# LayerNorm statistics in the feed-forward of a two-layer transformer stage: plain fp32 product against two fp32r products of a split sum

## The chip, the core and the metric

The kernel runs on one NeuronCore of a Trainium2 chip. Five engines work side by side from their own instruction queues and meet at semaphores: TensorE (PE: matrix products and transposes, into PSUM), VectorE (DVE), ScalarE (ACT), GpSimd (POOL) and SyncE (SP, which starts DMAs). The metric is the device time of one execution in microseconds (us), from the first to the last instruction and a little around it.

## The reference

The input is (2, 1024, 256), 2048 tokens of 256 features. The program computes a softmax attention with a field term, a quaternion rotation, a mixture over 64 experts, and then two layers of window attention and feed-forward. The change lies in the feed-forward of these last two layers. There the reference computes, for each token:

```
h = shift_token(x)
mu = h.mean(-1, keepdims=True)
var = h.var(-1, keepdims=True)
h = (h - mu) / jnp.sqrt(var + 1e-05) * lg + lb
h = h @ w1 + b1
a, g = jnp.split(h, 2, axis=-1)
h = a * jax.nn.gelu(g, approximate=False)
x = x + h @ w2 + b2
```

x has 256 columns, w1 is 256 x 1364 and w2 is 682 x 256.

## The kernel before, in words

Activations are kept transposed: features on the 128 partitions (two blocks, KD = 2), tokens along the free dimension. The feed-forward works in units of 512 tokens, four in each layer (UNITS = 4), so u = 0 to 3 is layer 0 and u = 4 to 7 is layer 1. In the texts "unit n" is the n-th unit of its layer, and it normalises ahead for unit n + 1.

The statistics of a unit of tokens need a sum over 256 features. VectorE first adds the two blocks of 128 features (`tile_sums`, L2008, and for the squares `square_sums`, L2023). Then TensorE multiplies the 128 x 512 result with a 128 x 128 matrix that holds 1/256 everywhere (`means`, L1576, and `variances`, L1580), which leaves the mean, or the variance, in every partition. In between, VectorE subtracts the mean (`centred`, L2017) and ScalarE squares (L1837). After the variance ScalarE takes the root (`deviation`, L1842), VectorE the reciprocal in two halves (`inverse`, L2029), GpSimd multiplies (`normalise`, L1464), ScalarE scales and shifts (L1851), VectorE takes the high part (L2034) and GpSimd the low part (L1470).

All large products of the feed-forward are made of three products of fp32r parts (PRODUCTS: high by high, low by high, high by low). For each of six tiles f of the hidden layer TensorE makes the gate and value products (`hidden`, L1635, 12 matmuls for a tile, 6 for the last), ScalarE the gelu (L1923), and VectorE a chain of three: the product with the gate (L2111), a cast to fp32r for the high part (L2114) and a subtraction for the low part (L2116). Two PSUM banks take turns for the tiles, so tile f waits until the L2111 of tile f - 2 is over. Then L1747 makes the second product in two pieces, tiles 0 to 3 and tiles 4 and 5. The last piece waits for the low part of tile 5. VectorE adds the result to x (L2138).

The order on each engine is that of the code, written out by hand:

- VectorE, unit n: `tile_sums(u + 1)`; tile 0 of the hidden layer, `centred(u + 1)`; tile 1, `square_sums(u + 1)`; tile 2; tile 3, first half of `inverse`; tile 4, second half; tile 5; the high part of unit n + 1; the two additions of L2138.
- TensorE, unit n: tile 0 (for unit 0 already within the attention); `means(u + 1)` ahead of tile 1; tiles 1 to 3; `variances(u + 1)`; tiles 4 and 5; L1747.
- GpSimd, between two units: normalise and low part, and then in unit 0 of layer 0 two long subtractions for the next layer's weights (`low_qkv`, L1452), in unit 1 the scaling of the tables (L1242), and in layer 1 the addition of the layer's input (`with_input`, L1477).

In the attention of each layer the first unit (u = 0 and u = 4) is normalised in other buffers (names n_... instead of m_...), among the attention's own work.

Of the kernel before, what the change touches and what calls it, by code (L numbers as in the profile page):

```python
# [22 lines left out]
F32 = mybir.dt.float32  # L23
F32R = mybir.dt.float32r
BF16 = mybir.dt.bfloat16
ACT = mybir.ActivationFunctionType
ALU = mybir.AluOpType
# [3 lines left out]
P = 128  # L31
B, T, D = 2, 1024, 256
N = B * T
KD = D // P
TT = T // P
HALF = 512
# [1216 lines left out]
def stage_layers(nc, G, A, out):  # L1253


    with ExitStack() as ctx:
        sb = lambda n, s, dt=F32: ctx.enter_context(nc.sbuf_tensor(n, s, dt))
        sem = lambda n: ctx.enter_context(nc.semaphore(n))
# [9 lines left out]
        UNITS = NH * B  # L1268
# [6 lines left out]
        rn = sb("w_rn", [P, 2, 2, 2 * H1])  # L1275
        st = sb("w_st", [P, 2, 4, H1])
        rden = sb("r_rden", [P, TILES])
        mean = sb("m_mean", [P, P])
        eps = sb("m_eps", [P, 1])


        with ExitStack() as place:
            own = lambda n, s, dt=F32: place.enter_context(nc.sbuf_tensor(n, s, dt))
# [11 lines left out]
            oT = own("w_oT", [P, 2, HP, P])  # L1295
        with ExitStack() as place:
            own = lambda n, s, dt=F32: place.enter_context(nc.sbuf_tensor(n, s, dt))
            xc = own("m_xc", [P, KD, HALF])
            sqr = own("m_sq", [P, KD, HALF])
            xsum = own("m_xsum", [P, HALF])  # L1300
            sqsum = own("m_sqsum", [P, HALF])
            sd = own("m_sd", [P, HALF])
            rs = own("m_rs", [P, HALF])
            xn = own("m_xn", [P, KD, HALF])
            hn = own("m_hn", [P, KD, HALF])
            own("m_gap", [P, 2, KD, HALF])
            x1o = own("m_x1T", [P, NH, KD, HALF])
            own("m_gap0", [P, 2 * INNER])
            own("m_gap1", [P, VRING, INNER])
            with ExitStack() as inner:  # L1310
                on = inner.enter_context(nc.sbuf_tensor("r_on", [P, 2, D], F32))
            hids = [own(f"m_hid_{c}", [P, FT, HALF], F32R) for c in range(2)]
            gl = own("m_gl", [P, 2, HALF])
            hid = own("m_hid", [P, 2, HALF])
            hn_odd = own("m_hn_1", [P, 2, KD, HALF], F32R)
# [8 lines left out]
        def of_norm(u):  # L1324

            if u % UNITS == 0:
                return xc_first, sqr_first, xsum_first, sqsum_first, sqsum_first, xsum_first, xc_first, sqr_first
            return xc, sqr, xsum, sqsum, sd, rs, xn, hn
# [9 lines left out]
        consts, mu_ps, xc_done, xq_done, var_ps, sd_done, rs_done, xn_done, hn_done, hn_high, hn_low = (sem("m_" + n) for n in (  # L1338
            "consts", "mu_ps", "xc_done", "xq_done", "var_ps", "sd_done", "rs_done", "xn_done", "hn_done", "hn_high", "hn_low"))
        h_ps, gl_done, hid_done, hid_high, hid_low, y_ps, y_done = (sem("m_" + n) for n in (  # L1340
            "h_ps", "gl_done", "hid_done", "hid_high", "hid_low", "y_ps", "y_done"))
        w_copy, w_low, w_round, xsum_done, sqsum_done, stored = (sem("m_" + n) for n in (
            "w_copy", "w_low", "w_round", "xsum_done", "sqsum_done", "stored"))
        ld_half = [sem(f"m_ld_half{hf}") for hf in range(NH)]
# [6 lines left out]
        def mean_banks(u):  # L1351

            return (V_PS, V_PS) if u % UNITS == 0 else (PB[1][:, 0:HALF], PB[1][:, HALF:2 * HALF])
# [20 lines left out]
        def halves_swapped(rows):  # L1374

            (part, count), (one, _) = rows.ap
            return bass.AP(rows.tensor, rows.offset + C * one,
                           [(part, count), (INNER * one, 2), (HD1 * one, H1), (-C * one, 2), (one, C)])

        def tokens_shifted(q):  # L1380

            rows = xr[:, 0, q // (NW // 2), :]
            (part, count), (one, _) = rows.ap
            return bass.AP(rows.tensor, rows.offset + (1 + 2 * P * (q % (NW // 2))) * one,
                           [(part, count), ((B * (1 + T) - 1) * one, KD), (one, 2 * P)])

        def shifted(n, k):
            c0 = n % NH * HALF + (1 if k == 0 else 0)
            return xr[:, k, n // NH, c0:c0 + HALF]
# [23 lines left out]
        with nc.Block() as block:  # L1413
# [32 lines left out]
            def _(pool):  # L1446
                V = nc.gpsimd
# [11 lines left out]
                def normalise(u):  # L1459
                    xc, _, _, _, _, rs, xn, _ = of_norm(u)  # L1460
                    pool.wait_ge(rs_done, 2 * (u + 1))
                    pool.wait_ge(hn_done, KD * u)
                    for k in range(KD):
                        V.tensor_tensor(xn[:, k, :], xc[:, k, :], rs[:, :], ALU.mult).then_inc(xn_done, 1)  # L1464
# [64 lines left out]
                            low_piece(l, t - 6)  # L1529

                V.memset(xr[:, :, :, 0:1], 0.0).then_inc(zeroed, 1)
                V.memset(mean[:, :], 1.0 / D).then_inc(consts, 1)
                V.memset(eps[:, :], LN_EPS).then_inc(consts, 1)
                pool.wait_ge(consts, 2)
                attention(0)
                normalise(1)
                norm_low(1)
# [15 lines left out]
            def _(pe):  # L1553
                mm, tr = nc.tensor.matmul, nc.tensor.transpose
# [9 lines left out]
                def rotate(n):  # L1564
                    pe.wait_ge(x1_done, 4 * n + 4)
                    for m in range(KD):
# [4 lines left out]
                                      start=(k == 0), stop=(k == KD - 1))  # L1571
                        last.then_inc(rot_ps, 1)

                def means(u):
                    pe.wait_ge(xsum_done, u + 1)
                    mm(mean_banks(u)[0], mean[:, :], of_norm(u)[2][:, :], start=True, stop=True).then_inc(mu_ps, 1)  # L1576

                def variances(u):
                    pe.wait_ge(sqsum_done, u + 1)
                    mm(mean_banks(u)[1], mean[:, :], of_norm(u)[3][:, :], start=True, stop=True).then_inc(var_ps, 1)  # L1580

                def project(l, out_ps, i, j):
                    for n, (ch, cw) in enumerate(PRODUCTS):
# [187 lines left out]
                pe.wait_ge(x1_done, TILES)  # L1771
                pe.wait_ge(rot_out, KD * (N // HALF))
                attention(0, EARLY_SLOTS)
                pe.wait_ge(consts, 2)
                feed_forward(0)
                attention(1, EARLY_SLOTS)
                feed_forward(1)
# [181 lines left out]
            def _(dve):  # L1959
                V = nc.vector  # L1960
# [34 lines left out]
                def inverse_norms(l, q):  # L1995
                    dve.wait_ge(n_sqrt, NG // 2 * l + q + 1)
                    dve.wait_ge(turn_done, NG * l + max(2 * q - 2, 0))
                    V.reciprocal(rn[:, q % 2, :, :], nrm[:, :, :]).then_inc(rn_done, 1)

                def tile_sums(u):  # L2000
                    l, n = u // UNITS, u % UNITS
                    dve.wait_ge(wo_done, NG * l + 4 * (n + 1))
                    dve.wait_ge(mu_ps, u)
                    if n == 0:
                        dve.wait_ge(xn_done, KD * u)
                    if n == 1:
                        dve.wait_ge(add_done, NG * (l + 1))
                    V.tensor_tensor(of_norm(u)[2][:, :], shifted(n, 0), shifted(n, 1), ALU.add).then_inc(xsum_done, 1)  # L2008

                def centred(u):  # L2010
                    dve.wait_ge(mu_ps, u + 1)
# [7 lines left out]
                def square_sums(u):  # L2019
                    dve.wait_ge(xq_done, KD * (u + 1))  # L2020
                    dve.wait_ge(var_ps, u)
                    _, sqr, _, sqsum, *_ = of_norm(u)
                    V.tensor_tensor(sqsum[:, :], sqr[:, 0, :], sqr[:, 1, :], ALU.add).then_inc(sqsum_done, 1)  # L2023

                def inverse(u, q):
                    dve.wait_ge(sd_done, u + 1)
# [146 lines left out]
def program(nc, A, out):  # L2173


    with ExitStack() as top:
# [76 lines left out]
        sb("weights_kept", [P, WEIGHTS])  # L2253
        moe.close()
        stage_layers(nc, G, A, out)


# [76 lines left out]
```

## Time and profile before

| | |
|---|---|
| three runs | 1533.12, 1534.72, 1535.19 us; median 1534.72 us |
| profiled execution, own time | 1532.85 us |
| its span | 1531.1 us, 24499 instructions |
| TensorE | busy 1465.6 us (96%), mean granted clock 0.992 |
| VectorE | busy 1033.9 us (68%) |
| ScalarE | busy 902.2 us (59%) |
| GpSimd | busy 495.1 us (32%) |

Busy time of TensorE is modelled up to the end of each matmul, which the next one overlaps: how fast the matmuls really follow each other is seen in the distance between the starts. The two feed-forward stages are at about 1100 to 1220 us and 1424 to 1531 us. A plain fp32 product of 128 x 128 by 128 x 512 stands in the trace as two matmul instructions with two weight loads, an fp32r product as one.

### The profile page before, as it was taken

How to read it: one execution, taken by the hardware profiler on the slowest of the kernel's cores; microseconds unless marked ns; L12 is line 12 of the kernel's file. 1: busy time of each engine (PE TensorE's matmuls, PEld its weight loads, DVE VectorE, ACT ScalarE, POOL GpSimd, SP SyncE). 2: the span in 40 equal slices, each digit the busy share in tenths (PEclk: the TensorE clock that was granted, in tenths of full speed). 3: DMA queues.
4: the chain of work that ended last, by engine and by line, in shares of the span. 5: the costliest groups of instructions: out<-in, count | busy, mean ns of one | idle time of the engine just before them, and what ended most of it. 6: DMA issues, size and time to landing. Idle time of an engine off the chain costs nothing. (4 is left out here: it accounts for less than half of the span.)

```text
span 1531.1 us, 24499 instructions
## 1 busy us (share of the span) xinstructions
PE 1465.6 (96%) x9004; PEld 960.0 (63%) x9004; DVE 1033.9 (68%) x1855; ACT 902.2 (59%) x1888; POOL 495.1 (32%) x323
## 2 busy tenths in 40 slices
PE   8889999999998899999999999999999899998998
PEld 3432222222224679888887668877777678887776
DVE  3768888888844455656565567776597577676685
ACT  5137777777775442534343278988543388987341
POOL 7200000000003410000004177887343378886222
PEclk9999999999999999999999999999999999999999
DMA  8930232110000313030305120000200100000010
GB/s 246 170 41 2 43 42 41 24 22 2 1 12 15 104 38 111 14 110 0 124 0 149 42 73 2 2 1 1 77 7 0 59 2 1 2 1 29 14 42 28
DMA packets 59477, 64.85 MB, mean 42 GB/s; under 512 B 15154, under 2 KB 48706, under 8 KB 59380
## 3 DMA queue, kind: packets, MB, share of 16 engines
q1 hardware_dynamic: 58020, 60.17, 15.7%
q10 hardware_dynamic: 1360, 3.41, 0.6%
q8 instruction: 58, 0.95, 0.3%
q14 instruction: 39, 0.32, 0.1%
HBM read 52.88 MB, written 10.49 MB: 41 GB/s over the span
## 5 line engine op out<-in xcount | busy, mean ns | idle before, releaser
L581 DVE TENSOR_REDUCE mcol<-bank 128x1 f32<-128x1024 f32 x256 | 302.1, 1217 | 56.5 <-PE bank L572 56.5
L669 ACT ACTIVATE a_pt<-bank 128x512 f32<-128x512 f32 x512 | 266.5, 602 | 89.1 <-PE bank L701 89.1
L701 PE MATMUL bank<-qa,ka 99*128 99x512 bf16 x512 | 193.7, 386 | 7.6 <-ACT a_pt L669 3.8
L572 PE MATMUL bank<-ka,qa 96*128 96x512 bf16 x512 | 192.7, 384 | 4.4 <-DVE mcol L581 1.4
L2045 DVE CUSTOM_DVE_ANT_0 w_sm<-bank,mask,w_rn 128x256 f32<-128x256 f32 (+1 forms) x256 | 104.1, 463 | 80.2 <-PE bank L1627 79.5
L701 PEld LDWEIGHTS bank<-qa,ka 99*128 99x128 bf16 x512 | 49.2, 98 | 165.7 <-ACT a_pt L669 121.3
L1585 PE MATMUL bank<-wqkv,w_hst 128*128 128x512 f32 x576 | 150.3, 405 | 2.7 <-DVE w_sinp L1984 2.3
L1878 ACT ACTIVATE w_sm<-w_sm,w_st 128x256 f32<-128x256 f32 (+1 forms) x256 | 124.2, 490 | 22.3 <-DVE w_st L2045 22.0
L712 PE MATMUL bank<-a_pt,vst 128*32 128x512 f32 x1024 | 136.4, 605 | 0.1
L1485 POOL TENSOR_TENSOR w_sm<-w_sm,w_st 128x1024 f32<-128x1024 f32 (+1 forms) x64 | 115.4, 1803 | 20.2 <-DVE w_st L2052 20.0
L1585 PEld LDWEIGHTS bank<-wqkv,w_hst 128*128 128x128 f32 x576 | 104.2, 189 | 25.8 <-issue 5.1
L618 POOL COPY vst<-v 128x512 f32<-128x512 f32 x8 | 4.9, 615 | 334.0 <-PE bank L712 279.5
L1076 PE MATMUL bank<-f_y,f_ET 128*128 128x256 f32 x768 | 108.7, 290 | 0.7 <-DVE f_y L1175 0.7
L1076 PEld LDWEIGHTS bank<-f_y,f_ET 128*128 128x128 f32 x768 | 96.1, 191 | 3.9 <-issue 1.6
L1033 PE MATMUL bank<-phi,X0T 128*128 128x512 f32 x384 | 92.1, 394 | 4.6 <-PEq L768 4.6
L1494 POOL TENSOR_TENSOR w_cosp<-w_qkr,cosT 128x1024 f32<-128x1024 f32 x32 | 76.5, 2392 | 54.2 <-ACT w_qkr L1815 27.2
L1007 PE MATMUL bank<-f_th,X 128*128 128x512 f32 x384 | 90.3, 389 | 0.0
L572 PEld LDWEIGHTS bank<-ka,qa 96*128 96x128 bf16 x512 | 49.7, 99 | 60.5 <-DVE mcol L581 11.3
L1033 PEld LDWEIGHTS bank<-phi,X0T 128*128 128x128 f32 x384 | 73.0, 191 | 20.6 <-issue 5.4
L1923 ACT ACTIVATE m_gl<-bank,b 128x512 f32<-128x512 f32 (+1 forms) x48 | 33.1, 689 | 85.8 <-PE bank L1635 85.7
L742 POOL CAST phi<-phi 128x1024 fp32r<-128x1024 f32 x5 | 5.2, 1042 | 240.3 <-PE bank L1033 150.5
L1007 PEld LDWEIGHTS bank<-f_th,X 128*128 128x128 f32 x384 | 72.1, 188 | 14.9
(254 smaller groups left out, 2846.4 us busy)
## 6 DMA issues: line engine op xcount, KB each, us to landing
f_wex<-in_W SPq DMA_DIRECT2D x8, 2048.0 KB, 12.1
qa<-q_parts SPq DMA_DIRECT2D x48, 128.0 KB, 4.7
ka<-k_parts SPq DMA_DIRECT2D x48, 128.0 KB, 5.0
q_parts<-p_parts SPq DMA_DIRECT2D x16, 192.0 KB, 3.2
k_parts<-p_parts SPq DMA_DIRECT2D x8, 384.0 KB, 3.4
wqkv_raw<-in_wqkv SPq DMA_DIRECT2D x2, 1536.0 KB, 6.9
w_raw<-in_w SPq DMA_DIRECT2D x2, 1408.0 KB, 5.9
phi<-in_phi SPq DMA_DIRECT2D x5, 512.0 KB, 3.8
```

Of the source, the lines that this page charges most:

```text
L572: last = nc.tensor.matmul(max_bank(G, r)[:, jh * HALF:(jh + 1) * HALF], G["qa"][k][0:KS, hg % 2, h, it * P:(it + 1) * P], G["ka"][k][0:KS, ...
L581: nc.vector.reduce_max(G["mcol"][hg % 2][:, p:p + 1], max_bank(G, r)[:, :], X).then_inc(G["max_free"], 1)
L669: nc.scalar.activation(pt[n % 2][:, q, :], sbank(HG * step + q), ACT.Exp, scale=HD0 ** -0.5).then_inc(p_ready, 1)
L701: mm(sbank(i), ka[k][:, q, n * P:(n + 1) * P], qa[k][:, ih, q, :], start=True, stop=True).then_inc(st_ps, 1)
L712: last = mm(obank[32 * q:32 * q + 32, :], vst[hg // 2 % 2][:, jt, q, :], pt[jt % 2][:, q, :], start=(jt == 0), stop=(jt == TT - 1))
L1007: last = mm(PB[2 + b][:, k * HALF:(k + 1) * HALF], X0[cx][:, b * TT + mt, k * P:(k + 1) * P], ths[ct][:, mt % 2, :], start=(mt == n == 0), ...
L1033: last = mm(logit_bank(mt)[:, b * HALF:(b + 1) * HALF], X0T[cx][:, k, b * T + mt * P:b * T + (mt + 1) * P], phis[cp][:, k, :], start=(n == ...
L1076: last = mm(PB[1][:, HALF * (t % 2):HALF * (t % 2) + D], ETs[ce][:, t % 2, n, :], ys[cy][:, n, t // TT, :], start=(n == i == 0), stop=(n = ...
L1485: V.tensor_tensor(sm[:, i % 2, hs, keys(i)], sm[:, i % 2, hs, keys(i)], st[:, i % 2, 3, hs].unsqueeze(2).to_broadcast([P, 4, 2 * WIN if i ...
L1585: last = mm(out_ps, hst[:, i // 2 % 2, ch, k, (i % 2) * P:(i % 2 + 1) * P], wqkv[cw][:, k, j * INNER:(j + 1) * INNER], start=(n == k == 0) ...
L1878: last = S(sm[:, i % 2, h, keys(i)], sm[:, i % 2, h, keys(i)], ACT.Exp, bias=st[:, i % 2, 1, h:h + 1], scale=-1.0, accum_out=st[:, i % 2, ...
L2045: V.tensor_tensor_reduce(sm[:, s, h, keys(i)], S_PS[h % 2][:, c0:c0 + 2 * WIN][:, keys(i)], mask_of(i), rn[:, i // 2 % 2, s, h:h + 1], HIG ...
```

## The change

For three units in each layer (all but the first, u % 4 > 0) the sum and the sum of squares are split on VectorE into a high part (cast to fp32r) and a low part (the sum minus the high part), and TensorE makes two fp32r matmuls that add up in PSUM instead of one fp32 matmul. Each of the new VectorE instructions waits by semaphore for the one ahead of it. The matrix of 1/256 becomes fp32r: GpSimd fills a scratch tile and copies it over, once. The first unit of each layer stays as it was. The parts lie in a buffer that was a gap.

```diff
@@ stage_layers
-        mean = sb("m_mean", [P, P])
+        mean = sb("m_mean", [P, P], F32R)
...
-            own("m_gap", [P, 2, KD, HALF])
+            sum_parts, square_parts = (own(f"m_{n}_parts", [P, 2, HALF], F32R) for n in ("sum", "square"))
@@ GpSimd
-                V.memset(mean[:, :], 1.0 / D).then_inc(consts, 1)
+                V.memset(oT[:, 0, 0, :], 1.0 / D).then_inc(consts, 1)
                 V.memset(eps[:, :], LN_EPS).then_inc(consts, 1)
                 pool.wait_ge(consts, 2)
+                V.tensor_copy(mean[:, :], oT[:, 0, 0, :]).then_inc(consts, 1)
@@ TensorE
+                def of_tokens(bank, u, whole, parts):
+                    if u % UNITS == 0:
+                        return mm(bank, mean[:, :].bitcast(F32), whole[:, :], start=True, stop=True)
+                    mm(bank, mean[:, :], parts[:, 0, :], start=True, stop=False)
+                    return mm(bank, mean[:, :], parts[:, 1, :], start=False, stop=True)
+
                 def means(u):
                     pe.wait_ge(xsum_done, u + 1)
-                    mm(mean_banks(u)[0], mean[:, :], of_norm(u)[2][:, :], start=True, stop=True).then_inc(mu_ps, 1)
+                    of_tokens(mean_banks(u)[0], u, of_norm(u)[2], sum_parts).then_inc(mu_ps, 1)
...
-                    mm(mean_banks(u)[1], mean[:, :], of_norm(u)[3][:, :], start=True, stop=True).then_inc(var_ps, 1)
+                    of_tokens(mean_banks(u)[1], u, of_norm(u)[3], square_parts).then_inc(var_ps, 1)
@@ VectorE
+                def in_parts(u, whole, parts, whole_done, high_done):
+                    v = u - u // UNITS
+                    dve.wait_ge(whole_done, v)
+                    V.tensor_copy(parts[:, 0, :], whole[:, :]).then_inc(high_done, 1)
+                    dve.wait_ge(high_done, v)
+                    return V.tensor_tensor(parts[:, 1, :], whole[:, :], parts[:, 0, :].bitcast(F32), ALU.subtract)
...
-                    V.tensor_tensor(of_norm(u)[2][:, :], shifted(n, 0), shifted(n, 1), ALU.add).then_inc(xsum_done, 1)
+                    whole = V.tensor_tensor(of_norm(u)[2][:, :], shifted(n, 0), shifted(n, 1), ALU.add)
+                    if n:
+                        whole.then_inc(sums_whole, 1)
+                        in_parts(u, of_norm(u)[2], sum_parts, sums_whole, sums_high).then_inc(xsum_done, 1)
+                    else:
+                        whole.then_inc(xsum_done, 1)
```

`square_sums` is changed in the same way.

VectorE, start of unit 1 of layer 0, up to the subtraction of the mean (m_xsum: sum over the two blocks; m_xc: after the mean is subtracted). Before:

```order
L2138 SCALAR_TENSOR_TENSOR xr<-bank,b,xr 128x512 x2
L2008 TENSOR_TENSOR m_xsum<-xr 128x512
L2111 SCALAR_TENSOR_TENSOR m_hid<-bank,b,m_gl 128x512
L2114 CAST m_hid<-m_hid 128x512
L2116 TENSOR_TENSOR m_hid<-m_hid 128x512
L2017 TENSOR_TENSOR m_xc<-xr,bank 128x512 x2
```

Now:

```order
L2166 SCALAR_TENSOR_TENSOR xr<-bank,b,xr 128x512 x2
L2026 TENSOR_TENSOR m_xsum<-xr 128x512
L2013 CAST m_sum_parts<-m_xsum 128x512
L2015 TENSOR_TENSOR m_sum_parts<-m_xsum,m_sum_parts 128x512
L2139 SCALAR_TENSOR_TENSOR m_hid<-bank,b,m_gl 128x512
L2142 CAST m_hid<-m_hid 128x512
L2144 TENSOR_TENSOR m_hid<-m_hid 128x512
L2040 TENSOR_TENSOR m_xc<-xr,bank 128x512 x2
```

The cast and the subtraction stand between the sum and tile 0's chain, and the mean's matmul is released by the subtraction, no longer by the sum.

TensorE, the same unit, between the end of tile 0 and the first products of tile 1 (w_0 and w_1: high and low part of w1). Before:

```order
L1635 MATMUL bank<-m_hn,w_0 128x512 x4
L1635 MATMUL bank<-m_hn,w_1 128x512 x2
L1576 MATMUL bank<-m_xsum,m_mean 128x512
L1635 MATMUL bank<-m_hn,w_0 128x512 x4
L1635 MATMUL bank<-m_hn,w_1 128x512 x2
```

Now:

```order
L1644 MATMUL bank<-m_hn,w_0 128x512 x4
L1644 MATMUL bank<-m_hn,w_1 128x512 x2
L1580 MATMUL bank<-m_sum_parts,m_mean 128x512
L1581 MATMUL bank<-m_sum_parts,m_mean 128x512
L1644 MATMUL bank<-m_hn,w_0 128x512 x4
L1644 MATMUL bank<-m_hn,w_1 128x512 x2
```

The place of the mean's product is the same; all products of tile 1 and after stand behind it in TensorE's queue, and so behind its wait.

## Rows read from the trace of the kernel before

**Rows 1.** Busy time: window, length, PE, PEld, DVE, ACT, POOL (counts), clock, DMA, GB/s

```profile
1127.42:1154.11 26.69, 26.54 (x106) 19.63 (x107) 23.77 (x28) 12.90 (x15) 12.02 (x8) 1.00 0.00 1
```

**Rows 2.** Chain that ended last, unit 0 of layer 0: start, us, what

```profile
1099.07 0.69 DVE m_xsum L2008
1099.77 0.14 issue
...
1109.49 0.76 DVE m_hid L2111
...
1118.42 1.68 DVE m_hid L2116
...
1120.14 3.63 PE bank L1747 x12
```

**Rows 3.** Timeline of TensorE's weight loads around L1580: start, us, operation, idle before

```profile
1108.99 0.42 PEld L1580 LDWEIGHTS bank<-m_sqsum,m_mean 128*128 128x128 f32 x2
1109.65 0.19 PEld L1635 LDWEIGHTS bank<-n_hn,w 128*128 128x128 f32 x1 [0.24 <-issue]
1110.08 3.90 PEld L1635 LDWEIGHTS bank<-n_hn,w 128*128 128x128 f32 x17 [0.24 <-issue]
```

**Rows 4.** Timeline of VectorE, layer 0

```profile
1100.45 0.43 DVE L2114 CAST m_hid<-m_hid 128x512 fp32r<-128x512 f32 x1
1100.91 0.69 DVE L2116 TENSOR_TENSOR m_hid<-m_hid 128x512 fp32r<-128x512 f32 x1
...
1124.47 2.80 DVE L2008 TENSOR_TENSOR m_xsum<-xr 128x512 f32<-128x512 f32 x1
...
1127.97 2.92 DVE L2114 CAST m_hid<-m_hid 128x512 fp32r<-128x512 f32 x1
...
1137.03 0.75 DVE L2111 SCALAR_TENSOR_TENSOR m_hid<-bank,b,m_gl 128x512 f32<-128x512 f32 x1
...
1152.00 1.82 DVE L2008 TENSOR_TENSOR m_xsum<-xr 128x512 f32<-128x512 f32 x1
```

**Rows 5.** Timeline of VectorE, layer 1

```profile
1448.76 0.68 DVE L2008 TENSOR_TENSOR m_xsum<-xr 128x512 f32<-128x512 f32 x1
1451.14 0.75 DVE L2111 SCALAR_TENSOR_TENSOR m_hid<-bank,b,m_gl 128x512 f32<-128x512 f32 x1 [1.69 <-PE bank L1635]
```

**Rows 6.** Timeline of GpSimd, layer 0

```profile
1123.22 7.39 POOL L1452 TENSOR_TENSOR wqkv<-wqkv_raw,wqkv 128x1536 fp32r<-128x1536 f32 x2
...
1153.23 1.72 POOL L1242 TENSOR_TENSOR cosT<-cosT,qks 128x512 f32<-128x512 f32 x1
1154.92 1.29 POOL L1242 TENSOR_TENSOR sinT<-sinT,qks 128x512 f32<-128x512 f32 x1
```

**Rows 7.** Timeline of GpSimd, layer 1

```profile
1448.92 1.68 POOL L1477 TENSOR_TENSOR m_x1T<-m_x1T,xr 128x512 f32<-128x512 f32 x1 [0.35 <-DVE xr L2138]
```

**Rows 8.** Timeline of TensorE, layer 0's feed-forward

```profile
1099.90 1.10 PE L1576 MATMUL bank<-m_xsum,m_mean 128*128 128x512 f32 x2 [1.21 <-DVE m_xsum L2008]
...
1123.69 3.05 PE L1635 MATMUL bank<-m_hn,w 128*128 128x512 f32 x12
...
1141.76 5.75 PE L1747 MATMUL bank<-m_hid,w 128*128 128x512 f32 x24
...
1154.11 1.02 PE L1576 MATMUL bank<-m_xsum,m_mean 128*128 128x512 f32 x2
...
1204.33 7.37 PE L1747 MATMUL bank<-m_hid,w 128*128 128x512 f32 x24 [2.01 <-DVE w_sinp L1984]
```

**Rows 9.** Timeline of TensorE, layer 0's attention

```profile
1068.70 2.07 PE L1627 MATMUL bank<-w_kT,w_qT 64*128 64x256 f32 x8 [2.32 <-ACT w_qT L1859]
```

**Rows 10.** Timeline of TensorE, layer 1

```profile
1394.17 1.13 PE L1627 MATMUL bank<-w_kT,w_qT 64*128 64x256 f32 x8 [2.32 <-ACT w_qT L1859]
...
1450.87 1.02 PE L1576 MATMUL bank<-m_xsum,m_mean 128*128 128x512 f32 x2
```

**Rows 11.** Busy time after the idle gap of 2.01 us, columns as rows 1

```profile
1206.00:1208.00 2.00, 2.00 (x6) 1.51 (x6) 0.16 (x1) 0.00 (x0) 1.70 (x2) 0.50 0.00 0
```

More of the change, by code:

```diff
@@ L1341, in stage_layers @@
             "h_ps", "gl_done", "hid_done", "hid_high", "hid_low", "y_ps", "y_done"))
+        sums_whole, sums_high, squares_whole, squares_high = (sem("m_" + n) for n in (
+            "sums_whole", "sums_high", "squares_whole", "squares_high"))
         w_copy, w_low, w_round, xsum_done, sqsum_done, stored = (sem("m_" + n) for n in (
@@ L1773, in _ @@
                 attention(0, EARLY_SLOTS)
-                pe.wait_ge(consts, 2)
+                pe.wait_ge(consts, 3)
                 feed_forward(0)
@@ L2004, in tile_sums @@
                     if n == 0:
+                        dve.wait_ge(consts, 3)
                         dve.wait_ge(xn_done, KD * u)
@@ L2022, in square_sums @@
                     _, sqr, _, sqsum, *_ = of_norm(u)
-                    V.tensor_tensor(sqsum[:, :], sqr[:, 0, :], sqr[:, 1, :], ALU.add).then_inc(sqsum_done, 1)
+                    whole = V.tensor_tensor(sqsum[:, :], sqr[:, 0, :], sqr[:, 1, :], ALU.add)
+                    if u % UNITS:
+                        whole.then_inc(squares_whole, 1)
+                        in_parts(u, sqsum, square_parts, squares_whole, squares_high).then_inc(sqsum_done, 1)
+                    else:
+                        whole.then_inc(sqsum_done, 1)
                 def inverse(u, q):
```

## The prediction

> **What bounds the kernel now.** I read the chain of waits first, then the timelines of the three engines around the mean's product. TensorE is busy in 26.54 of the 26.69 us from one mean's product to the next, VectorE in 23.77 [rows 1], so the feed-forward looks like TensorE's. The chain says it is shared: sum on VectorE, mean and tiles 1 to 3 on TensorE, then from 1109.49 to 1120.1 VectorE alone (tiles 3, 4, 5 and two reciprocals), then the last piece of L1747 [rows 2]. So in every unit with a next one two things end last: how early tile 3's products are over, and what VectorE does from there to the low part of tile 5.
>
> **What TensorE saves.** In a steady run 17 weight loads of fp32r matmuls take 3.90 us from the first start to the last end; less the last one's 0.19, over 16 distances, that is 0.23 us each. The two loads of the fp32 variance begin at 1108.99 and end at 1109.41, so the second starts at about 1109.22; the next start at 1109.65 and 1110.08, so each of its two matmuls holds the engine for 0.43 us [rows 3]. Two fp32r matmuls take 0.47 us instead of 0.86, 0.39 us less. Twelve products: 4.7 us less work.
>
> The six variances save nothing of the end: they stand behind tile 3 of TensorE, and from tile 3 on the chain runs on VectorE, up to the point where L1747 waits for it [rows 2]. What TensorE wins there it waits for before the last piece. The six means stand ahead of tile 1 and count, if VectorE is in time.
>
> **What VectorE adds.** A cast of 128x512 takes 0.43 us and a subtraction 0.69 us in tile 0's chain; the second starts 0.03 us after the first's end [rows 4]. Behind a sum, with 0.04 us for the first wait: 1.19 us, twelve times, 14.3 us more on VectorE, and each mean's product is released that much later, at least. Queued behind the cast and the subtraction are tile 0's chain and the subtraction of the mean; queued behind TensorE's wait is tile 1 and all that follows.
>
> The six splits of the squares are hidden, as long as VectorE has idle time left (2.9 of 26.7 us in rows 1's window, the fullest): TensorE takes the variance only behind tile 3, and tile 3's chain starts when its products are over [rows 2], so what the split after tile 1 delays on VectorE has two tiles of TensorE to be caught up. I count nothing, with up to 0.3 us each as the other end, 1.8 us.
>
> **The sums, unit by unit.** Tile 3's chain starts 9.59 us after the mean's product (1099.90 [rows 8], 1109.49 [rows 2]); with fp32r 9.20.
>
> Unit 0, in both layers (layer 1's has the same idle 1.21 us): the sum ends at 1099.76, TensorE starts 0.14 us after it [rows 2] and waited 1.21 us for it [rows 8]. Later by 1.19, less 0.39: +0.8 each, 1.6 us.
>
> Unit 1 of layer 0: GpSimd has two long subtractions of together 7.39 us, from 1123.22 to 1130.61 [rows 6]. VectorE's sum falls on the first and takes 2.80 us instead of 0.69, and tile 0's cast on the second: 2.92 us instead of 0.43, over at 1130.89 [rows 4]. Both end shortly after a GpSimd instruction does.  Now the new cast comes at 1127.31, just after the second one has begun. It ends when tile 0's cast did, at about 1130.9, the subtraction at 1131.6, and TensorE starts at 1131.76 instead of 1127.42. Tile 3's chain then starts at 1131.76 + 9.20 = 1140.96 instead of 1137.03 [rows 4]: +3.9. Tile 0's cast, no longer blocked, gives nothing back, because it now comes behind. Without blocking the unit would cost 0.8; the longest it can cost is 0.8 plus both new instructions waiting for a GpSimd instruction of 3.5 us, about 6.
>
> The Trainium skill (SBUF — State Buffer, section "SBUF: two separate sides") says that a VectorE instruction with two SBUF inputs or in a two-port mode and a GpSimd instruction lock one pair of ports for their whole length, and that the one that comes later is blocked fully, not slowed. By that rule the new cast waits for all the rest of GpSimd's subtraction, as I took it; were the ports only shared in proportion, the unit would cost nearer to 2 us. The rows of the 2.80 and the 2.92 us agree with the rule.
>
> Unit 2 of layer 0: the sum starts at 1152.00 and ends at 1153.82 [rows 4]. GpSimd's scaling runs from 1153.23 to 1154.95, then from 1154.92 to 1156.21 [rows 6]. The new cast waits for the first (to about 1155.25), which pushes the second on by 0.3 us, and the new subtraction for the second: 1156.5, over at about 1157.05. TensorE starts at 1157.2 instead of 1154.11 [rows 8]: 3.1, less 0.4, +2.7. Unblocked, the subtraction would be over at 1155.0 and the unit cost 0.7.
>
> Units 1 and 2 of layer 1: the sum ends at 1449.44, TensorE starts at 1450.87 without a wait, so there is slack of 1.29 us [rows 5, 10], a little more than the 1.19 us. But GpSimd's addition, from 1448.92 to 1450.60 [rows 7], blocks the cast to about 1450.9; subtraction over at 1451.6, TensorE at 1451.75: +0.9, less 0.39: +0.5 each, 1.0 us. Unblocked they would gain 0.39 each. Tile 0's chain had 1.69 us of idle ahead of it [rows 5], so it isn't held much.
>
> Sum of the waits: 1.6 + 3.9 + 2.7 + 1.0 = 9.2 us.
>
> **What the longer gaps do to TensorE's clock.** After the gap of 2.01 us before 1204.33, the granted clock fell to 0.50, the lower level of 1.2 GHz [rows 11], and 24 matmuls of L1747 took 7.37 us instead of 5.75 [rows 8], 1.6 us more. After a gap of 2.32 us eight matmuls took 2.07 us [rows 9], after another gap of 2.32 us 1.13 us [rows 10]: it does not happen each time. No row shows a fall after 1.21 us. The new gaps are 1.21 + 1.19 = 2.4 us twice (unit 0), about 2.9 us (unit 2) and, since tile 0's products are over at 1126.74 [rows 8], 5.0 us (unit 1). I take the two longer ones and one of the 2.4 us as falls, at 1.3 us each (1.6 from the row, less where the low clock covers a part of the gap itself): 3.9 us. Bounds: none, and four at 1.6, 6.5 us.
>
> What else is new costs nothing that shows: one small copy on GpSimd at the stage's start, far ahead of the first split.
>
> **Sum.** 9.2 + 3.9 = 13.1 us on the profiled execution's 1532.85 gives 1545.9; the median of the runs shown is 1.9 us higher, so 1547.8 on that. I say 1547.
>
> **Rivals.**
> 1. *The ports don't block the new instructions as I read it* (the cast slips in between two of GpSimd's). For it: the sums of rows 4 did get in between two. Against: the cast comes some 40 ns behind the sum, and GpSimd's next one is queued since before. Then 1.6 + 0.8 + 0.7 - 0.8 = 2.3 us, and one fall of the clock or two, 1.3 to 2.6: about 1539.
> 2. *The clock stays up.* For it: one of the gaps of 2.32 us left it. Against: three of the four new gaps would have to be spared, one of them 5.0 us. 1534.7 + 9.2: 1544.
> 3. *The bound is VectorE throughout.* Then the square splits, 1.19 us each, are on the path too in the units where VectorE has no gap left (units 1 and 2 of layer 0): 2.4 us more, 1550. Against: tile 1's chain waits for products that come later as well.
> 4. *Not slower.* Mechanism: TensorE is the only bound and the split lies in VectorE's idle time, so that the 0.39 us of all twelve products come off the end, -4.7 us: 1530. For it: TensorE is busy 96%, VectorE 68%. Its place is the start of the mean's product, its price the 1.19 us, and it decides where the slack ahead of that is over 1.19 us. Only two of the six means have 1.29 us, the others none, and the variances' gain is taken by the wait before L1747's last piece. A variant, that the split doesn't make the product faster (two fp32r matmuls at 0.43 us), would add 0.39 us at six means, 2.3 us.
>
> **How the numbers follow.** Forecast 0.55 (1547, own spread 1543 to 1551), rival 1 0.16, rival 2 0.14, rival 3 0.08, rival 4 0.03, the rest for what I haven't seen. The range 1539 to 1551 takes in rivals 1 to 3. What a measurement of this kernel can tell from no change is about 0.2%, 3 us. Slower by more: the forecast, rivals 2 and 3, most of rival 1: 0.90. Within: 0.07. Faster: 0.03.
>
> **What the profile after would show.** Right: two matmuls of the parts with loads 0.23 us apart; idle before the mean's product of about 2.4 us in unit 0 of both layers, 5 us and 3 us in units 1 and 2 of layer 0, 0.7 us in layer 1's; a cast of the sum's parts of about 3.5 us in unit 1; granted clock of 0.5 behind some of these gaps; the wait before L1747's last piece longer by up to 0.4 us. Wrong: if the new cast takes 0.43 us everywhere, or if the time between a mean's product and the next grows by other amounts than the idle time before it.

## The result and the profile after

The change makes the kernel slower: 1548.21 us (median of four runs, 1546.61 to 1549.52) against 1534.95 us for the kernel before (1533.12 to 1535.79), a ratio of 1.0089 with a 95% interval of 1.0077 to 1.0102. That is 13.3 us by the medians and 13.7 us by the ratio. The profiled execution took 1546.61 us with a span of 1544.8 us, against 1532.85 and 1531.1 us.

In the changed kernel the sum is L2026, the cast L2013 and the subtraction L2015 of `in_parts`; L2139, L2142 and L2144 are the chain of a tile, L1644 is `hidden`, L1580 and L1581 are the two matmuls of a mean or a variance, L1756 is the second product, and GpSimd's long subtractions are L1454.

The most useful measure is the unit period: from the start of one unit's sum on VectorE to the next's (for a unit 2, to the start of the second addition to x). Read from the timeline of VectorE, in us; in brackets for how long the granted clock was 0.5, added up from the mean clock of pieces of 1 us:

| | before | after |
|---|---|---|
| start to unit 0 of layer 0 | 1099.07 | 1102.36 |
| layer 0, unit 0 | 25.40 (0) | 27.52 (3.4) |
| layer 0, unit 1 | 27.53 (0) | 32.45 (3.4) |
| layer 0, unit 2 | 25.95 (0) | 29.83 (3.4) |
| from there to unit 0 of layer 1 | 245.41 (3.4) | 243.77 (0) |
| layer 1, unit 0 | 25.40 (0) | 25.93 (0) |
| layer 1, unit 1 | 26.60 (0) | 26.93 (0) |
| layer 1, unit 2 | 25.94 (0) | 26.25 (0) |
| rest | 29.80 | 29.76 |
| the six units | 156.82 | 168.91 |

The six units took 12.1 us more. The 3.3 us ahead of them and the 1.6 us less between the layers lie where the change touches next to nothing; over the twelve profiles of this study the start of unit 0 lies anywhere from 1099.1 to 1103.8 us and the stretch between the layers takes 243.8 to 246.6 us, whatever the kernel; no part of that is counted to the change. The stretch between the layers goes with its low clock: 243.8 us in the three profiles without any, 245.0 to 245.4 in the five with 3.4 us of it, 246.2 to 246.6 in the four with 6.8. And products_alone (below), which has the change's matrix and buffers, starts unit 0 at 1099.21 us, as before.

These are the periods in the windows view of the kernel after (window, length, busy time and count of PE, PEld, DVE, ACT, POOL, then granted clock, DMA share, GB/s), to be held against [rows 1]:

```profile
1102.36:1129.88 27.52, 25.18 (x97) 19.13 (x98) 22.51 (x34) 12.12 (x14) 6.71 (x5) 0.94 0.42 115
1129.88:1162.33 32.45, 27.18 (x107) 20.45 (x106) 27.72 (x33) 12.81 (x15) 12.77 (x8) 0.95 0.00 1
1162.33:1192.16 29.83, 26.75 (x105) 20.04 (x103) 24.88 (x32) 10.06 (x13) 9.81 (x8) 0.94 0.00 1
1435.93:1461.86 25.93, 23.61 (x97) 17.96 (x98) 22.48 (x34) 9.37 (x12) 6.50 (x5) 1.00 0.00 1
1461.86:1488.79 26.93, 25.90 (x107) 19.47 (x106) 23.48 (x34) 10.06 (x13) 8.18 (x6) 1.00 0.11 40
```

VectorE is now busy in 27.72 of 32.45 us in unit 1, TensorE no longer all the time. The clock is 0.94 to 0.95 in the three units of layer 0 and 1.00 in layer 1. The chain that ended last, in unit 0 of layer 0 (start, us, what), answers to [rows 2]:

```profile
1102.36 0.69 DVE m_xsum L2026
...
1103.08 0.44 DVE m_sum_parts L2013
...
1103.54 0.70 DVE m_sum_parts L2015
1104.24 0.14 issue
1104.38 0.47 PE bank L1580
1104.84 0.23 PE bank L1581
1105.07 4.37 PE bank L1644 x12
...
1115.10 0.76 DVE m_hid L2139
...
1123.82 1.68 DVE m_hid L2144
...
1125.55 3.64 PE bank L1756 x12
```

Two VectorE steps, 0.44 and 0.70 us, have come between the sum and the mean's product. Between 1105.07 and 1115.10 us the chain goes through the split of the squares (1112.11 us) as well: from the start of tile 1's chain to that of tile 3's TensorE's two tiles take 5.57 us, and VectorE's work, with that split, 5.49 (squares_only below, 1136.43 to 1141.92, where nothing holds it). So that split fits in with less than 0.1 us to spare. The pair of fp32r matmuls is shorter, as predicted against [rows 3]: weight loads of the variance 0.23 us apart, and the next one 0.23 us behind.

```profile
1114.61 0.19 PEld L1580 LDWEIGHTS bank<-m_square_parts,m_mean 128*128 128x128 f32 x1
1114.84 0.19 PEld L1581 LDWEIGHTS bank<-m_square_parts,m_mean 128*128 128x128 f32 x1
1115.07 4.14 PEld L1644 LDWEIGHTS bank<-n_hn,w 128*128 128x128 f32 x18
```

TensorE's timeline shows the gaps, in layer 0 (answering to [rows 8]) and in layer 1 (to [rows 10]):

```profile
1104.38 0.47 PE L1580 MATMUL bank<-m_sum_parts,m_mean 128*128 128x512 f32 x1 [2.39 <-DVE m_sum_parts L2015]
...
1125.55 3.62 PE L1756 MATMUL bank<-m_hid,w 128*128 128x512 f32 x12 [0.32 <-DVE m_hid L2144]
...
1137.11 0.77 PE L1580 MATMUL bank<-m_sum_parts,m_mean 128*128 128x512 f32 x1 [4.95 <-DVE m_sum_parts L2015]
...
1167.38 0.77 PE L1580 MATMUL bank<-m_sum_parts,m_mean 128*128 128x512 f32 x1 [2.78 <-DVE m_sum_parts L2015]
...
1218.54 5.82 PE L1756 MATMUL bank<-m_hid,w 128*128 128x512 f32 x24 [2.01 <-DVE w_sinp L1993]
```

```profile
1437.94 0.47 PE L1580 MATMUL bank<-m_sum_parts,m_mean 128*128 128x512 f32 x1 [2.39 <-DVE m_sum_parts L2015]
...
1464.85 0.47 PE L1580 MATMUL bank<-m_sum_parts,m_mean 128*128 128x512 f32 x1 [0.72 <-DVE m_sum_parts L2015]
```

The waits for the sum's parts are 2.39, 4.95 and 2.78 us in layer 0, 2.39 and 0.72 us in layer 1. The last row of the first block is the place where before's clock had fallen: 24 matmuls now take 5.82 us, not 7.37. And this is where the two longer waits come from, on VectorE ([rows 4, 5]) and on GpSimd ([rows 6]):

```profile
1129.88 2.79 DVE L2026 TENSOR_TENSOR m_xsum<-xr 128x512 f32<-128x512 f32 x1
1132.71 3.52 DVE L2013 CAST m_sum_parts<-m_xsum 128x512 fp32r<-128x512 f32 x1
1136.27 0.69 DVE L2015 TENSOR_TENSOR m_sum_parts<-m_xsum,m_sum_parts 128x512 fp32r<-128x512 f32 x1
...
1162.33 1.82 DVE L2026 TENSOR_TENSOR m_xsum<-xr 128x512 f32<-128x512 f32 x1
1164.19 1.38 DVE L2013 CAST m_sum_parts<-m_xsum 128x512 fp32r<-128x512 f32 x1
1165.60 1.63 DVE L2015 TENSOR_TENSOR m_sum_parts<-m_xsum,m_sum_parts 128x512 fp32r<-128x512 f32 x1
```

```profile
1462.58 1.40 DVE L2013 CAST m_sum_parts<-m_xsum 128x512 fp32r<-128x512 f32 x1
```

```profile
1128.61 7.33 POOL L1454 TENSOR_TENSOR wqkv<-wqkv_raw,wqkv 128x1536 fp32r<-128x1536 f32 x2
```

A cast that takes 0.43 us alone takes 3.52 us in unit 1, up to 1136.23, where GpSimd's two instructions run from 1128.61 to 1135.94; 1.38 us in unit 2, with a subtraction of 1.63 us behind it; and 1.40 us in layer 1's units.

### The profile page after: what moved, and what is told of

The parts are those of the page before. It is cut to its first block and busy times, and to the rows that moved or that the text cites. A ratio compares the mean times of both kernels' runs of the same rounds, so it can differ in the third digit from the quotient of the medians.

```text
span 1544.8 us, 24526 instructions
## 1 busy us (share of the span) xinstructions
PE 1465.8 (95%) x9004; PEld 962.8 (62%) x9004; DVE 1049.6 (68%) x1879; ACT 901.3 (58%) x1888; POOL 494.9 (32%) x324
```

## The experiments

Each median is set against runs of the kernel before on the same chip; the unit periods come from each kernel's profile, without the brackets. All edits are against the changed kernel, and the line numbers move a little with each edit (the chain of a tile is L2134, L2137 and L2139 in squares_only):

| | ratio to before (95%) | six units | L0: 0, 1, 2 | L1: 0, 1, 2 |
|---|---|---|---|---|
| before | | 156.8 | 25.40, 27.53, 25.95 | 25.40, 26.60, 25.94 |
| after | 1.0089 (1.0077 to 1.0102) | 168.9 | 27.52, 32.45, 29.83 | 25.93, 26.93, 26.25 |
| squares_only | 1.0013 (1.0003 to 1.0024) | 156.9 | 25.18, 28.46, 25.89 | 25.15, 26.38, 25.88 |
| sums_only | 1.0105 (1.0090 to 1.0120) | 172.7 | 27.57, 33.41, 30.08 | 27.68, 27.16, 26.84 |
| products_alone | 0.9983 (0.9974 to 0.9991) | 153.5 | 24.75, 27.34, 25.31 | 24.79, 25.98, 25.30 |
| splits_alone | 1.0105 (1.0087 to 1.0122) | 175.5 | 28.15, 34.35, 30.52 | 28.05, 27.57, 26.90 |
| filled_gaps | 1.0052 (1.0039 to 1.0065) | 164.5 | 25.90, 31.20, 28.34 | 25.89, 26.93, 26.27 |
| plain_in_2_3 | 1.0033 (1.0021 to 1.0044) | 161.6 | 27.45, 27.51, 25.94 | 27.50, 26.94, 26.26 |
| gpsimd_pieces | 1.0075 (1.0062 to 1.0088) | 165.5 | 25.99, 30.56, 29.83 | 25.93, 26.96, 26.26 |
| squares_pieces | 0.9996 (0.9988 to 1.0005) | 156.0 | 25.16, 27.52, 25.89 | 25.16, 26.38, 25.88 |
| squares_but_2 | 0.9995 (0.9986 to 1.0004) | 154.9 | 25.16, 26.60, 25.90 | 25.16, 26.37, 25.70 |
| squares_but_2_filled | 0.9991 (0.9982 to 1.0000) | 154.9 | 25.17, 26.60, 25.88 | 25.16, 26.37, 25.70 |

**One part at a time.** First the squares alone.

```diff
-                    of_tokens(mean_banks(u)[0], u, of_norm(u)[2], sum_parts).then_inc(mu_ps, 1)
+                    mm(mean_banks(u)[0], mean[:, :].bitcast(F32), of_norm(u)[2][:, :], start=True, stop=True).then_inc(mu_ps, 1)
...
-                        in_parts(u, of_norm(u)[2], sum_parts, sums_whole, sums_high).then_inc(xsum_done, 1)
```

> Only the squares are split, the means are plain fp32 products again. Theory (all of the loss sits in the sums' splits, which hold TensorE back ahead of tile 1, and the variance's shorter product gives about 0.2 us a unit, as the stretch from tile 3's L2139 to the end of the last L2144 went from 10.65 to 10.45 us): 6 x 0.2 = 1.2 us less than before, 1533.8 us; idle before the mean's product back to 1.2 us in unit 0. Rival A (VectorE is full in units 1 and 2 of layer 0, so each square's split of 1.19 us is paid there): 2.4 us more than before or beyond, 1537.5. Rival B (the prediction's count, variances give nothing): 1535.0.

Median 1536.28 us. The longer wait before the means is gone as expected (1.21 us again in unit 0), and so is nearly the whole loss, but the expected gain isn't there. The periods say why: 0.2 us less in units 0 of both layers and unit 1 of layer 1, only 0.06 us less in the two units 2, and 0.93 us more in unit 1 of layer 0. There VectorE goes from one instruction to the next without any idle time:

```profile
1136.43 0.74 DVE L2134 SCALAR_TENSOR_TENSOR m_hid<-bank,b,m_gl 128x512 f32<-128x512 f32 x1
...
1138.28 0.68 DVE L2041 TENSOR_TENSOR m_sqsum<-m_sq 128x512 f32<-128x512 f32 x1
1139.00 0.43 DVE L2013 CAST m_square_parts<-m_sqsum 128x512 fp32r<-128x512 f32 x1
1139.46 0.69 DVE L2015 TENSOR_TENSOR m_square_parts<-m_sqsum,m_square_parts 128x512 fp32r<-128x512 f32 x1
1140.07 0.74 DVE L2134 SCALAR_TENSOR_TENSOR m_hid<-bank,b,m_gl 128x512 f32<-128x512 f32 x1
```

From the sum at 1128.19 to the last cast at 1152.19 no row of VectorE has idle time ahead of it. So the square's split, 1.2 us, is paid there, less what the variance gives. Both rivals were wrong too: A put that price in two units (its total, 2.4 us more than before, lies within the measured interval, its places don't fit), B put nothing anywhere. The six units sum to 156.94, before's to 156.82; the measured 0.5 to 3.7 us more than before lies, as far as it is over that, outside the units, and was not located.

```diff
-                    of_tokens(mean_banks(u)[1], u, of_norm(u)[3], square_parts).then_inc(var_ps, 1)
+                    mm(mean_banks(u)[1], mean[:, :].bitcast(F32), of_norm(u)[3][:, :], start=True, stop=True).then_inc(var_ps, 1)
...
-                        in_parts(u, sqsum, square_parts, squares_whole, squares_high).then_inc(sqsum_done, 1)
```

> Only the sums are split, the variances are plain fp32 products again. Theory: the whole loss stays and the variances' 1.2 us go, 1548.2 + 1.2 = 1549.4 us; the cast of the sum's parts still takes about 3.5 us in unit 1 of layer 0. Rival A (squares' splits cost 2.4 us): 1545.8. Rival B: 1548.2.

Median 1550.71 us, by the ratio 16.1 us over before (13.8 to 18.4). The theory's 1549.4 is within that, rival A's 1545.8 is not: the loss is all in the sums. The cast of unit 1 takes 3.52 us again. This profile has a fall of the clock in unit 0 of layer 1 as well (27.68), and 6.8 us of low clock in unit 1 of layer 0, which the change's own profile had not.

**The two halves of the idea, each alone.** Products without splits:

```diff
-                    whole = V.tensor_tensor(of_norm(u)[2][:, :], shifted(n, 0), shifted(n, 1), ALU.add)
...
+                    dst = sum_parts[:, 0, :] if n else of_norm(u)[2][:, :]
+                    V.tensor_tensor(dst, shifted(n, 0), shifted(n, 1), ALU.add).then_inc(xsum_done, 1)
...
-                    return mm(bank, mean[:, :], parts[:, 1, :], start=False, stop=True)
+                    return mm(bank, mean[:, :], parts[:, 0, :], start=False, stop=True)
```

> The fp32r products without the split: VectorE writes the sum itself as fp32r, with no cast and no subtraction, and both matmuls read that one part (the low part is left out and the high part counted twice, so mean and variance come out doubled). Theory: the two fp32r matmuls save 0.39 us at five of six means (not in unit 1 of layer 0, where VectorE is as late) and 0.2 us at six variances: 3.2 us less than before, 1531.8. Rival (TensorE's work counts in full, 12 x 0.39): 1530.3. Rival (nothing of it reaches the end): 1535.

Median 1532.18 us; by its ratio 2.6 us less than before (1.4 to 4.0), and 3.35 us less in the six units. That is near the theory's 3.2 and not the 4.7 us of TensorE's work. Where nothing else is in the way (layer 1) a unit gives 0.61 to 0.64 us, the mean's 0.39 and the variance's 0.2; in unit 1 of layer 0 it gives 0.2. So a split pays only if it costs less than some 3 us in all.

```diff
-                    of_tokens(mean_banks(u)[0], u, of_norm(u)[2], sum_parts).then_inc(mu_ps, 1)
+                    mm(mean_banks(u)[0], mean[:, :].bitcast(F32), of_norm(u)[2][:, :], start=True, stop=True).then_inc(mu_ps, 1)
```

(and the variance likewise; the splits stay, and what TensorE waits for)

> The splits without the fp32r products: VectorE casts and subtracts as in the change and TensorE waits for it, but multiplies the whole sum in fp32 as before. Theory: the change's loss of 13.3 us plus what the products gave back, 3.2 us: 16.5 us over before, 1551.5. Rival (the extra VectorE work costs no more than its own 14.3 us, all of it on the path, without falls of the clock): 1549.3, and then the granted clock in the gaps stays 1.00.

Median 1549.51 us. The ratio makes it 16.1 us over before (13.4 to 18.7), for 16.5 expected; the time alone doesn't part the theory from the rival's 14.6 us more. The clock does: it falls, which the rival excluded. Its six runs lie in two groups, four at 1548.0 to 1549.7 and two at 1555.5 and 1555.9; the profile is of the second, with 17.1 us of low clock in the six units.

**The gaps filled.** TensorE keeps on working while it waits for the sum's parts:

```diff
+                FILL = {1: 9, 2: 20, 3: 11, UNITS + 1: 9}
+
                 def means(u):
+                    for _ in range(FILL.get(u, 0)):
+                        mm(mean_banks(u)[0], w1s[0][:, 0, 0:P], hns(u - 1)[:, 0, 0, :], start=True, stop=True)
                     pe.wait_ge(xsum_done, u + 1)
```

> The change, with extra fp32r matmuls on TensorE ahead of its wait for the mean's sum (9 in unit 0 of both layers, 20 in unit 1 and 11 in unit 2 of layer 0), whose result is overwritten. Theory: the idle gaps cost twice, once as waiting and once as low clock behind them; the extra matmuls only fill the gap (2.1, 4.7 and 2.6 us of 2.4, 5.0 and 2.8) and keep the clock up. Unit periods of layer 0: 27.5 to 25.9, 32.5 to 31.1, 29.8 to 28.3 us, granted clock 1.00 in them: 4.4 us less than the change, about 1544. Rival (the low clock only covers waiting that is there anyway): unit periods as with the change, 1548.

Median 1541.8 us, ratio 1.0052. TensorE's timeline and the clock of unit 1's period:

```profile
1129.51 4.82 PE L1587 MATMUL bank<-m_hn,w 128*128 128x512 f32 x20
1134.63 0.50 PE L1580 MATMUL bank<-m_sum_parts,m_mean 128*128 128x512 f32 x1 [0.30 <-DVE m_sum_parts L2019]
```

```profile
1127.40:1158.60 31.20, 30.57 (x127) 1.00 0.00 1
```

Twenty useless matmuls, still a wait of 0.30 us behind them, and the unit is 1.25 us shorter; units 0 and 2 of layer 0 by 1.62 and 1.49. In sum 4.4 us, as expected, and the clock is 1.00 throughout the six units. The unit 0 of layer 1, which had no fall in the change's profile, is unchanged (25.89 for 25.93). So the gaps are paid once as waiting and once as slow matmuls behind them. The median fell by more, 5.7 us by the ratios. That other executions have falls that the one profiled had not, as sums_only's profile has, would explain it; it is not shown for these.

**The change without the two units where GpSimd blocks.** `of_tokens`, `tile_sums` and `square_sums` take the old way for u = 2 and 3.

```diff
-                    if u % UNITS == 0:
+                    if u % UNITS == 0 or u in (2, 3):
```

> The change everywhere but for the statistics that units 1 and 2 of layer 0 make ahead (u = 2 and 3), which are plain fp32 again. Theory (the loss sits where GpSimd blocks the cast): unit 1's period falls from 32.5 to before's 27.5 us, unit 2's from 29.8 to 26.0: 8.8 us less, 1539.4. Rival (each of the six splits costs about the same, 13.3 / 6 = 2.2 us): 4.4 us less, 1543.8.

Median 1539.55 us, for 1539.4 by the theory and 1543.8 by the rival. Two of the six units make three fifths of the loss (8.6 of 13.7 us by the ratios); their periods are before's again (27.51, 25.94). This profile has a fall of the clock in both units 0 (27.45 and 27.50 us).

**GpSimd's instruction cut in three.**

```diff
-                    V.tensor_tensor(low, G["wqkv1_raw"][:, k, :], low.bitcast(F32), ALU.subtract).then_inc(G["wqkv_low"], 1)
+                    for c in range(3):
+                        cs = slice(c * INNER, (c + 1) * INNER)
+                        last = V.tensor_tensor(low[:, cs], G["wqkv1_raw"][:, k, cs], low[:, cs].bitcast(F32), ALU.subtract)
+                    last.then_inc(G["wqkv_low"], 1)
```

> The change, with each of GpSimd's two 128x1536 subtractions of the next layer's weights made in three pieces of 128x512. Theory (a VectorE instruction waits for the end of the GpSimd instruction that has the port): the sum, cast and subtraction of unit 1 wait for some 1.2 us each at most instead of up to 3.5: cast 1.4 us instead of 3.52, subtraction up to 1.9 instead of 0.69, sum 1.8 instead of 2.79; TensorE's gap 5.0 to 3.5 us, unit 1's period 32.5 to some 30.5, total 1546. Rival (VectorE is slowed by all of GpSimd's work in proportion, whatever its length): cast and period unchanged.

VectorE, then GpSimd:

```profile
1129.31 1.82 DVE L2029 TENSOR_TENSOR m_xsum<-xr 128x512 f32<-128x512 f32 x1
1131.17 1.38 DVE L2016 CAST m_sum_parts<-m_xsum 128x512 fp32r<-128x512 f32 x1
1132.58 1.63 DVE L2018 TENSOR_TENSOR m_sum_parts<-m_xsum,m_sum_parts 128x512 fp32r<-128x512 f32 x1
```

```profile
1128.04 8.74 POOL L1456 TENSOR_TENSOR wqkv<-wqkv_raw,wqkv 128x512 fp32r<-128x512 f32 x6
```

Sum 1.82, cast 1.38, subtraction 1.63 us: what VectorE waits for is the GpSimd instruction that is running, so its length matters, and not GpSimd's load, which is the same work (six instructions now end 8.74 us after the first start, against 7.33). TensorE's wait is 2.78 us instead of 4.95 (3.5 were expected), the period 30.56 us, expected 30.5; the rival, no change, is out. Median 1545.1 us; its ratio of 1.0075 and the change's 1.0089 have overlapping intervals, so the case rests on these rows. Unit 0 of layer 0 has no fall of the clock in this profile, after the same gap of 2.39 us (25.99 for 27.52 us); that part of the smaller sum is not the pieces' doing.

**Towards a version that is faster than both.** The splits that VectorE can hide are the squares', so: squares only, with GpSimd's pieces.

```diff
+                    for c in range(3):
+                        cs = slice(c * INNER, (c + 1) * INNER)
+                        last = V.tensor_tensor(low[:, cs], G["wqkv1_raw"][:, k, cs], low[:, cs].bitcast(F32), ALU.subtract)
```

(in squares_only)

> Only the squares are split (means plain fp32, as in the first of these experiments) and GpSimd's long subtractions are in three pieces. Theory: in unit 1 of layer 0 VectorE has idle time again (sum about 1.8 instead of 2.8 us, tile 0's cast about 1.5 instead of 2.9), so the square's split is hidden: period 28.46 to about 26.7 us, below before's 27.53; the other units as in squares_only. Over all units 155.2 us against before's 156.8: 1.6 us less, 1533. Rival (unit 1 is bound by something else than the blocked instructions): period stays at 28.4.

Median 1533.86 us, ratio 0.9996: not to be told from before. The period of unit 1 went down by 0.9 us, but to 27.52, not 26.7: VectorE's sum, cast and subtraction there still wait, and behind 1131.34 VectorE has no idle time up to the end of tile 5's chain.

```profile
1128.95 1.82 DVE L2029 TENSOR_TENSOR m_xsum<-xr 128x512 f32<-128x512 f32 x1
1131.34 0.75 DVE L2137 SCALAR_TENSOR_TENSOR m_hid<-bank,b,m_gl 128x512 f32<-128x512 f32 x1 [0.57 <-PE bank L1647]
1132.12 1.31 DVE L2140 CAST m_hid<-m_hid 128x512 fp32r<-128x512 f32 x1
1133.47 1.67 DVE L2142 TENSOR_TENSOR m_hid<-m_hid 128x512 fp32r<-128x512 f32 x1
```

Next, the square of u = 2 as before as well, in fp32:

```diff
-                    if u % UNITS:
+                    if u % UNITS and u != 2:
                         whole.then_inc(squares_whole, 1)
```

> The squares are split and multiplied as fp32r in five units only, not in the statistics that unit 1 of layer 0 makes ahead (u = 2); means plain fp32; GpSimd's long subtractions in three pieces. Theory (each square's split costs nothing where VectorE has idle time, and 0.9 us where it has none): unit 1's period from 27.52 (squares split there too, pieces) to about 26.8 us; all six periods together 155.3 us against before's 156.8: 1.5 us less than before, about 1533.1. Rival: unit 1 stays at 27.5 and the sum is 156.0.

Unit 1 takes 26.60 us, as the theory says, and the six units 154.9, 1.9 us less than before's. The ratio is 0.9995 (0.9986 to 1.0004), again not to be told from before. And eight filling matmuls in a gap of 2.0 us between the layers, which the kernel before has too:

```diff
                         if ahead:
+                            pe.wait_ge(sd_done, u + 1)
+                            for _ in range(8):
+                                mm(PB[1][:, HALF:2 * HALF], w1s[0][:, 0, 0:P], hns(u)[:, 0, 0, :], start=True, stop=True)
                             pe.wait_ge(qk_sb, NG * (l + 1) + EARLY_SLOTS)
```

> The same, with eight extra fp32r matmuls (results unused) in TensorE's gap of 2.0 us ahead of L1747 in unit 3 of layer 0, behind which the clock fell in the profile of before. Theory: the 24 matmuls behind it take 5.8 instead of 7.4 us in the executions that had the fall: 1.6 us less where it came, some 1.0 us less in the median, about 1532. Rival (the fall moves to another place): the same as without.

Median 1533.46 us, ratio 0.9991 with an interval that ends at 1.0000. It is the fastest version that computes all of the reference, 1.4 us below before by its ratio, but not shown beyond doubt to beat it. The fall behind the gap is gone, but the stretch between the layers takes 246.24 us, for 246.54 without the filling, and has 6.8 us of low clock in both profiles. Without it, 3.4 us lie behind the gap (the 24 matmuls take 7.37 us) and 3.4 us in layer 1's attention; with it, all 6.8 us lie in layer 1's attention, from the end of the gap of the second row on:

```profile
1205.63 5.82 PE L1762 MATMUL bank<-m_hid,w 128*128 128x512 f32 x24
...
1393.87 2.08 PE L1639 MATMUL bank<-w_kT,w_qT 64*128 64x256 f32 x8 [2.31 <-ACT w_qT L1874]
```

In these two profiles it is as the rival says, the low clock came in another place. With one profile of each it is not shown that it always does.

## Why the prediction came out right, step by step

**What bounds the kernel, and TensorE's saving.** Right for the means: 0.39 us of a product reach the end if VectorE is in time (products_alone). The time from the mean's product to tile 3's chain, forecast as 9.20 us, is 9.17 in unit 0 of layer 1 (1437.94 to 1447.11), where the clock stayed up. Wrong for the variances, "save nothing of the end". They give 0.2 us each: from tile 3's L2139 to the last piece of L1756 it was 10.65 us [rows 2] and is 10.45 (1115.10 to 1125.55), in every unit, and TensorE's wait before that piece grew only from 0.15 to 0.32 us, where up to 0.4 more was forecast. The step that failed is that the chain from tile 3 on is VectorE alone. Two distances in it shrank by 0.11 us each: from the first reciprocal to tile 4's L2139 (1.78 to 1.67 us) and from there to the second reciprocal (1.86 to 1.75; L2139 itself takes 0.65 us for 0.75). ScalarE's timeline has the wait behind it, first before, then after:

```profile
1110.28 0.69 ACT L1842 ACTIVATE m_sd<-bank,m_eps 128x512 f32<-128x512 f32 x1 [0.27 <-PE bank L1580]
...
1112.29 0.69 ACT L1923 ACTIVATE m_gl<-bank,b 128x512 f32<-128x512 f32 x1
```

```profile
1115.64 0.69 ACT L1851 ACTIVATE m_sd<-bank,m_eps 128x512 f32<-128x512 f32 x1
...
1117.64 0.69 ACT L1932 ACTIVATE m_gl<-bank,b 128x512 f32<-128x512 f32 x1
```

Before, ScalarE's root waited 0.27 us for the variance, and the gelu of tile 4 stands behind the root. It was over at 1112.98, and tile 4's L2111 started at 1113.13, 0.15 us later. In all six units the root has these 0.27 us and L2111 starts 0.15 to 0.16 us after the gelu's end, so it is L2111 that waited for the gelu (inferred from these times; VectorE's row names no wait). Now the root waits for nothing, the gelu is over at 1118.33 and L2139 starts 0.30 us later, right behind the reciprocal. So the path ran from the variance over ScalarE to tile 4's chain, and a shorter variance product did reach the end. In six units that is 1.2 us.

**The splits on VectorE.** The 1.19 us between sum and product is there in both units 0: the wait went from 1.21 [rows 8] to 2.39 us, 1.18 more.

**The squares' splits are hidden.** Right in the change, with less than 0.1 us to spare in a unit, and in unit 1 of layer 0 only because TensorE comes later still there (VectorE has 1.99 us of idle time ahead of tile 1's chain); by itself one of them costs 0.93 us net (squares_only, unit 1 of layer 0). The bound of 0.3 us given for it was too narrow, and rival 3's reason was sound in one unit of the two.

**The sums, unit by unit.** Without the clock's share the forecast was +0.8, +3.9, +2.7 in layer 0 and +0.8, +0.5, +0.5 in layer 1. With the gaps filled, so without falls, the units are +0.50, +3.67, +2.39, +0.49, +0.33 and +0.33 over before. All six forecasts are 0.2 to 0.3 us too high, 1.5 us in sum, and the variance's 0.2 us in each is most of what was missing. The blocked casts: predicted to end when tile 0's cast had, measured 3.52 us (some 3.5 said), and the whole chain in unit 2 as worked out. Gaps of 2.4, 5.0 and 2.9 us were forecast, 2.39, 4.95 and 2.78 measured. The Trainium skill (SBUF — State Buffer, section "SBUF: two separate sides") has the later one of a VectorE and a GpSimd instruction on the same pair of ports fully blocked until the other instruction ends; the runs agree, 3.52 us behind a 128x1536 instruction and 1.38 us behind a 128x512 one.

**The clock.** Three falls at 1.3 us were forecast, 3.9 us. The profile has three. These are stretches of 2 us shortly behind a gap (busy TensorE, then granted clock), three in layer 0 and one in layer 1:

```profile
1106.00:1108.00 2.00, 2.00 (x6) 0.50 0.97 399
1138.00:1140.00 2.00, 2.00 (x6) 0.52 0.00 0
1168.00:1170.00 2.00, 2.00 (x6) 0.50 0.00 0
1438.00:1440.00 2.00, 2.00 (x9) 1.00 0.00 0
```

The first three, behind the gaps of layer 0, are at 0.50 to 0.52, the lower level of 1.2 GHz; the fourth is behind the gap of 2.39 us of layer 1, as long as the first one's, and stayed at 1.00. The three falls cost 4.4 us together, 1.62, 1.25 and 1.49 us. Each is 3.4 us of low clock; in unit 1 about 0.6 us of that lies in the gap itself, where it costs nothing. That one of the two gaps of 2.39 us would have a fall and the other not was a guess between the bounds, and the count of three came out by luck: in sums_only, splits_alone and plain_in_2_3 both had one, in gpsimd_pieces neither.

**The sum.** 9.2 + 3.9 = 13.1 us were forecast; in the six units 12.1 were found, made of 7.7 (the filled version) and 4.4. Two errors of size partly cancel: the waits were forecast 1.5 us too high (1.2 of it the variances' gain, taken as nothing) and the clock's share 0.5 too low. By the ratios instead of the profiles, the filled version is 8.0 us over before and the falls are worth 5.7, which would make the clock's share 1.8 us too low; these have intervals of some 2 us either side, so it is a hint only. So the mechanism of the waits was right, and the closeness of 1547 to 1548.21 is partly luck. That the measured median is 13.3 us up and not 12.1 is within what the rest of the program varies by.

Rival 1 (not blocked), rival 2 (clock stays up) and rival 4 (hidden) are each refuted by a row above: 3.52 us, 0.50, and the idle of 2.39 us. Rival 3 (the squares' splits on the path in units 1 and 2 of layer 0) is refuted for the change by VectorE's idle time there ahead of tile 1's chain, 1.99 and 2.19 us. Rival 4's other form, fp32r no faster, is refuted by the weight loads.

## What to carry to other kernels

Price a cheaper product with what makes its operands, and at the place where the consumer waits: here 0.39 us of TensorE was bought with 1.19 us ahead of a wait that had no slack. Look which VectorE instructions fall beside a long GpSimd instruction. Here the sum, the cast and the subtraction, whose operands all lie in SBUF, had to wait for it, and the product with the gate, which reads PSUM too, took its 0.75 us beside it (squares_pieces, 1131.34, with GpSimd at its pieces from 1127.68 to 1136.29). A new instruction of the first kind costs the rest of GpSimd's, and shorter pieces on GpSimd make it cheaper. Gaps of 2.0 us and more on TensorE were followed by slow matmuls in many profiles here and not in all, at 1.3 to 1.6 us each; price a new gap of that length with and without it.

## What was not expected

The low clock around the gap of 5 us came in two amounts: 3.4 us of it in the change's unit 1, but 6.8 us in that unit of sums_only and splits_alone. One and the same program took 1547.97 to 1555.93 us (splits_alone); that such falls in other places make the difference is likely, but only one of its runs was profiled. A change of a microsecond is seen in the unit periods of one profile (without a fall of the clock, a unit with the same code repeats within 0.2 us from kernel to kernel), not in the medians.
